# A graph network layer on one core: raw groups behind every second chunk of x, and SP fetching one tile of 48 by byte addresses

## The chip, the cores and the metric

The kernel runs on one core of a Trainium2 chip. The metric is device time in microseconds of one execution of the whole program on that core. Engines are PE (TensorE), DVE (VectorE), ACT (ScalarE), POOL (GpSimd) and SP (SyncE); in the profile a "q" behind an engine's name is its sequencer or queue (SPq: what SP issues).

## The reference

`x` has 12,500 rows of 256 features; there are 212,500 edges, sorted by `dst`, each with a source row `src` and 64 features of its own. All is float32.

```python
h = relu(layernorm(x))                                   # no scale or bias
messages = concat([h[src], edge_attr], axis=1) @ W_message   # 320 -> 256
agg = segment_sum(messages, dst)
n = layernorm(relu(agg) + h) * scale + bias
n = n + relu(n @ W0 + b0); n = n + relu(n @ W1 + b1); n = n + (n @ W2 + b2)
out = x + layernorm(h + n) * scale2 + bias2
```

## The kernel before, in words

**Tiles.** Nodes are 98 blocks of 128. Edges are 1,661 tiles of 128 edges, in 208 groups of 8 tiles (`G`). For a tile, 128 rows of `h` (1 KB each) are fetched by `src` into a slot of `ring` (64 slots, 8 groups, `RG`), with the 64 edge features beside them; PE multiplies the tile (128 x 320) by a one-hot matrix that DVE makes from `dst` and adds it to the block's sum in `acc_banks` (L628). When a block ends, about every 17 tiles, PE makes a visit (L519): the sums are multiplied by `W_message` and the block goes on through the layers, with DVE (L814) and ACT (L692).

**First stage.** x comes in 14 chunks of 896 KB (7 blocks each). DVE takes mean and variance (`x_moments`, L1030), ACT the root and then the normalised, rectified rows (`x_root`, `x_to_h`, L750 and L756), and SP stores the chunk to `h_table` in HBM (L370). The first four chunks are staged in the ring's upper half, the others in the five buffers of `xs`. Gathers from `h_table` can start only when all chunks are stored. Therefore the first 10 groups ("raw", `RAWS`) are gathered by POOL from x itself, 8 into the ring and 2 ("extra") into `xs` when its chunks are gone (L440), and are normalised in place, as units of the same pipeline. `UNITS` (L54) is the order: before, raw groups stand behind chunks 5 to 11 and 13, and two more at the end; 24 units. Beside the units DVE and ACT prepare the keys of the edges (`parts`, L1128; `keys`, L780). In its first stage SP asks for chunk n + 3 when chunk n is stored (L373).

**Main loop.** For the other groups each tile's rows come in one of two ways. POOL issues one indirect gather of 128 rows for a tile (`gather`, L433); its groups stand in the program one behind another. For the last tile of every eighth group, one tile of 64, SP fetches the rows: 128 single-row loads of 1 KB (L401), whose row numbers it loads into 32 registers four times (L398, L327). Those numbers are taken from `src` by 24 small loads before the loop (L391). SP also loads each group's edge features (`load_edges`, L340), which waits until PE has freed enough groups (`group_free`). A round of SP is eight edge loads and one tile of rows, 24 rounds (`MID`); then six groups ("tail") follow. POOL, too, waits for `group_free` before a group (L469). PE waits for each pair of tiles by `gathered`, for SP's tile by four semaphores `rows_in`, and for the edge features by `edges_in`. DVE waits for `group_free` before it makes the one-hots of a group two ahead.

**Order.** Each engine runs its own list in order; POOL's software queue q0, SP's queue q1 and ACT's q10 share 16 DMA engines. The end, for the last blocks, is written out (`pe_end`, L534; `act_end`; `dve_end`) and begins behind the last group.

Of the kernel before, what the change touches and what calls it, by code (L numbers as in the profile page):

```python
# [8 lines left out]
I32 = mybir.dt.int32  # L9
ALU = mybir.AluOpType  # L10
# [3 lines left out]
P = 128  # L14
D = 256
# [3 lines left out]
G = 8  # L19
# [3 lines left out]
BY_ROW = 32  # L23
XS = 5
# [15 lines left out]
def build(nc, x, src, dst, edges, w_message, w_mlp, feature_params, row_params, out, NB, XB, T):  # L40
# [44 lines left out]
    with ctx:  # L85
# [34 lines left out]
        xs = sb("xs", [P, XS, XB, D])  # L120
# [3 lines left out]
        xs_flat = xs[:, :, :, :].rearrange("p s b d -> p (s b d)")  # L124
        extra = xs_flat[:, 0:max(EG, 1) * G * F].rearrange("p (t f) -> p t f", f=F)
        rows_flat = xs_flat[0:1, 3 * XB * D:3 * XB * D + ROUNDS * P].bitcast(I32)
# [9 lines left out]
        row_src = rows_flat.rearrange("a (i p) -> a i p", p=P)  # L136
# [130 lines left out]
        rows_in = [sem(f"rows_in{c}") for c in range(P // BY_ROW)]  # L267
# [68 lines left out]
        def _(sp):  # L336
# [91 lines left out]
        def _(pool):  # L428
# [142 lines left out]
        def _(pe):  # L571
# [11 lines left out]
            def group(p, i, k, fetched, tiles=G):  # L583

                offset = {"raw": 0, "extra": RG, "SP": EG, "tail": EG, "later": 0}[fetched]
                g = i * RG + k + offset
# [3 lines left out]
                rhs = extra if fetched == "extra" else ring  # L590

                uses = i if fetched in ("SP", "tail") else (p - 1) * ROUNDS + i + 1 + MID + (1 if k < TAIL else 0)
                if fetched == "extra":
                    pe.wait_ge(extra_edges_in[k], 16)
                elif fetched == "raw":
                    pe.wait_ge(edges_in[k], 16)
                else:
                    pe.wait_ge(edges_in[k], (uses + 1) * 16)
# [4 lines left out]
                def rows_of(j):  # L603

                    slot = k * G + j
                    pair = slot // PT
# [6 lines left out]
                    if slot % PT:  # L613
                        return
                    if fetched == "SP" and pair == RG * PAIRS - 1:
                        pe.wait_ge(gathered[pair], uses * (16 * (PT - 1)))
                        return

                    short = 0
                    if k == TAIL - 1 and fetched != "SP":  # L620
                        short += PT - min(max(ENDS - j, 0), PT)
                    if pair == RG * PAIRS - 1:
                        short += MID
                    pe.wait_ge(gathered[pair], uses * (16 * PT) - short * 16)

                def tile(j):
                    at = steered[j]
                    return nc.tensor.matmul(acc_of(at), onehot[:, hot + j, :], rhs[:, k * G + j, :],  # L628
                                            start=False, stop=True, skip_group_check=True)

                def close():
                    pe.wait_ge(close_ready, visit + 1)
                    at = steered[AT]
                    sel = steered[VSEL]
                    closing = rhs[:, bass.ds(at + k * G, 1), :].rearrange("p a f -> p (a f)")
                    nc.tensor.matmul(acc_of(sel), close_hot[:, :], closing, start=False, stop=True,  # L636
                                     skip_group_check=True).then_inc(block_closed, 1)
# [23 lines left out]
            with nc.Fori(1, MID + 1, engines=[mybir.EngineType.PE], hint_back_edge=True) as i:  # L661
                for k in range(RG):
                    group(0, i, k, "SP")
            for k in range(TAIL):
                group(0, MID + 1, k, "tail", ENDS if k == TAIL - 1 else G)
# [82 lines left out]
        def _(act):  # L748
# [24 lines left out]
            def wrong_keys():  # L773
                act.wait_ge(rel_ready, 1)
                nc.scalar.activation(rel[:, :], rel[:, :], ACT.Relu, bias=highest[:, 0:1],
                                     accum_out=wrong[:, 0:1]).then_inc(wrong_ready, 1)
                nc.scalar.activation(below[:, :], below[:, :], ACT.Relu, scale=-1.0,
                                     accum_out=wrong[:, 1:2]).then_inc(wrong_ready, 1)
# [196 lines left out]
        def _(dve):  # L975
# [54 lines left out]
            def x_moments(u):  # L1030
# [8 lines left out]
                left = [] if u == 0 else list(range(5))  # L1039
                for k in range(count):  # L1040
                    rows_at = staged(n)[:, k, :] if kind == "chunk" else raw_tile(n, k)[:, 0:D]
                    op = nc.vector.bn_stats(x_stats[:, u % 2, k, :], rows_at)  # L1042
                    if k == count - 1:
                        op.then_inc(x_stats_ready, 1)
                    if u >= 1 and k == 0:
# [6 lines left out]
            def x_finish():  # L1052
                x_aggregate(len(UNITS) - 1)
                for k in range(5):
                    x_scale(len(UNITS) - 1, k)
# [15 lines left out]
            def check_keys():  # L1071
                dve.wait_ge(blocks_ready, 1)
                dve.wait_ge(dst_ready, 1)
                nc.vector.scalar_tensor_tensor(rel[:, :], blk[:, 1:T + 1], -float(P), dst_f[:, :], ALU.mult, ALU.add)
# [161 lines left out]
```

## Time and profile before

| | |
|---|---|
| median of 3 runs | 2134.97 us (2129.38 to 2136.38) |
| the profiled execution | 2135.35 us |
| its span, first to last instruction | 2133.5 us |
| mean granted TensorE clock | 0.905 |
| busy: PE, POOL, DVE, ACT | 1609.0, 1572.2, 967.5, 408.4 us |
| indirect gathers of POOL | 1,637 (80 from x, 1,557 from `h_table`) |
| single-row loads of SP | 3,072 (24 tiles) |

The span is followed from the first to the last instruction; the profiled time is 1.85 us longer. Times in the rows below are microseconds from the span's start, means and minima marked ns are nanoseconds. A busy share is an average over the stages; the first stage lasts to about 127 us, the main loop from there to about 2098, and the end to 2133.5.

### The profile page before, as it was taken

The page shows a single profiled execution, that of the slowest core. Times are in us where ns is not written, and L with a number is a line of the kernel's source. Part 1 is how long each engine was busy: PE and PEld are TensorE (multiplying, and loading weights), DVE is VectorE, ACT ScalarE, POOL GpSimd, SP SyncE. Part 2 cuts the span into 40 slices and gives each one's busy share as a digit, 9 for nine tenths or more (in the row PEclk, how much of TensorE's full clock was granted, in tenths as well). Part 3 has the DMA queues.
Part 4 walks back from the last instruction along what each step waited for, and adds up shares of the span by engine and source line. Part 5 has one row for each costly group of instructions (what it writes and reads, how often), then busy time and mean ns, then how long its engine had stood idle before and what let it go on. Part 6 is the DMA issues. An engine that isn't in the chain of part 4 may idle for free.

```text
span 2133.5 us, 41823 instructions
## 1 busy us (share of the span) xinstructions
PE 1609.0 (75%) x6722; PEld 1119.5 (52%) x6723; DVE 967.5 (45%) x4162; ACT 408.4 (19%) x1209; POOL 1572.2 (74%) x1645
## 2 busy tenths in 40 slices
PE   0059796697778769769769787878887887878886
PEld 0047574475456557547546555545555554545554
DVE  7866453353344344335335334434343434433445
ACT  5852111121111111111111111111111111111112
POOL 7657777777777777777777777777777777777772
PEclk9989997898888889879889889999999999999988
DMA  9796466556646646655664664665566466566461
GB/s 384 249 247 187 139 174 166 142 163 171 166 135 174 166 137 176 165 152 155 168 165 143 165 169 135 172 166 158 146 173 162 138 168 163 145 165 163 140 188 55
DMA packets 369326, 357.18 MB, mean 167 GB/s; under 512 B 256288, under 2 KB 312672, under 8 KB 369152
## 3 DMA queue, kind: packets, MB, share of 16 engines
q0 software_dynamic: 78576, 214.67, 35.3%
q1 hardware_dynamic: 233984, 89.44, 17.1%
q10 hardware_dynamic: 56592, 51.54, 7.7%
q14 instruction: 160, 1.31, 0.2%
q8 instruction: 14, 0.23, 0.0%
HBM read 329.01 MB, written 26.48 MB: 167 GB/s over the span
## 4 chain that ended last, share of the span: by engine, by line
POOL 42%; SPq 23%; issue 21%; PE 7%; DVE 2%; DMA 2%; ACT 2%; DVEq 0%; POOLq 0%; ACTq 0%
POOL ring L435 42%; SPq L401 16%; SPq L327 4%; PE acc_banks L628 3%; SPq L342 2%; ACT xs L761 1%; SPq L328 1%; PE agg_bank L504 1%; DMA xs<-x 1%; PE agg_bank L509 1%; PE y_bank L492 1%; DVE x_stats L1042 1%; ACT ring L761 1%; PE z_bank L492 1%; POOL xs L447 0%
## 5 line engine op out<-in xcount | busy, mean ns | idle before, releaser
L435 POOL DMA_INDIRECT ring<-h_table,src_all x1557 | 1491.7, 958 | 488.1 <-issue 471.8
L628 PE MATMUL acc_banks<-ring,onehot 128*128 128x320 f32 x3290 | 1027.4, 463 | 330.6 <-DMA ring<-h_table,src_all 161.2
L628 PEld LDWEIGHTS acc_banks<-ring,onehot 128*128 128x128 f32 x3290 | 634.2, 201 | 683.7 <-issue 487.7
L1159 DVE TENSOR_SCALAR onehot<-iota,dst_rel 128x128 f32<-128x128 f32 x1664 | 350.2, 296 | 353.0 <-PE acc_banks L628 325.4
L825 DVE TENSOR_TENSOR visit_rows<-agg_bank,visit_rows 128x256 f32<-128x256 f32 x98 | 41.6, 424 | 722.9 <-PE agg_bank L509 715.2
L678 ACT ACTIVATE uT<-z_bank,fp 128x128 f32<-128x128 f32 x196 | 78.9, 453 | 1266.4 <-PE z_bank L498 1261.5
L504 PE MATMUL agg_bank<-wm,ST 128*128 128x256 f32 (+1 forms) x582 | 172.0, 418 | 0.0
L504 PEld LDWEIGHTS agg_bank<-wm,ST 128*128 128x128 f32 (+1 forms) x582 | 110.7, 203 | 59.6 <-issue 40.0
L498 PE MATMUL z_bank<-ident,z 128*128 128x128 f32 x196 | 41.6, 297 | 104.5 <-DMA ring<-h_table 103.5
L684 ACT ACTIVATE r_bank<-y_bank,fp 128x128 f32<-128x128 f32 x196 | 58.6, 337 | 297.8 <-PE y_bank L492 297.8
L509 PE MATMUL agg_bank<-wl,u 128*128 128x256 f32 x392 | 114.5, 416 | 0.0
L492 PEld LDWEIGHTS y_bank<-u,wl 128*128 128x128 f32 x784 | 106.5, 198 | 5.8 <-issue 0.3
L492 PE MATMUL y_bank<-u,wl 128*128 128x128 f32 x784 | 106.9, 281 | 0.0
L492 PE MATMUL z_bank<-uT,wl 128*128 128x128 f32 x784 | 105.6, 279 | 0.0
L498 PEld LDWEIGHTS z_bank<-ident,z 128*128 128x128 f32 x196 | 29.3, 155 | 130.9 <-issue 114.0
L492 PEld LDWEIGHTS z_bank<-uT,wl 128*128 128x128 f32 x784 | 97.8, 196 | 0.0
L509 PEld LDWEIGHTS agg_bank<-wl,u 128*128 128x128 f32 x392 | 68.4, 195 | 39.1 <-issue 33.5
L435 POOL DMA_INDIRECT ring<-x,src_all x64 | 64.6, 1010 | 20.6 <-issue 19.2
L636 PE MATMUL acc_banks<-ring,close_hot 128*128 x192 | 75.6, 479 | 0.0
L684 ACT ACTIVATE r_bank<-z_bank,fp 128x128 f32<-128x128 f32 x196 | 58.6, 337 | 30.5 <-PE z_bank L492 27.8
L842 DVE TENSOR_TENSOR u<-u,r_bank 128x256 f32<-128x256 f32 x98 | 40.8, 416 | 17.9 <-ACT r_bank L684 17.1
L515 PE MATMUL st_bank<-ident,S_cur 128*128 128x128 f32 (+1 forms) x294 | 48.2, 273 | 0.0
(173 smaller groups left out, 1089.0 us busy)
## 6 DMA issues: line engine op xcount, KB each, us to landing
ring<-edges SPq DMA_DIRECT2D x206, 256.0 KB, 6.0
ring<-h_table SPq DMA_DIRECT2D x3072, 1.0 KB
ring<-h_table,src_all POOLq DMA_INDIRECT x1557
h_in<-h_table ACTq DMA_DIRECT2D x98, 128.0 KB
visit_rows<-h_table ACTq DMA_DIRECT2D x98, 128.0 KB
visit_rows<-x ACTq DMA_DIRECT2D x98, 128.0 KB
out<-o ACTq DMA_DIRECT2D x93, 128.0 KB
xs<-x SPq DMA_DIRECT2D x10, 896.0 KB, 10.8
```

The source lines that it names most:

```text
L327: eng.load(regs, table[0:1, bass.ds(start, len(regs))])
L401: sp.dma_start(ring[lane_at:lane_at + 1, RT - 1, 0:D], h_table[bass.ds(at[q], 1), :]).then_inc(rows_in[c], 16)
L435: nc.gpsimd.indirect_dma_start(out=ring[:, k * G + j, 0:D], out_offset=None, in_=rows, in_offset=bass.IndirectOffsetOnAxis(ap=src_all[:, g ...
L492: mm = nc.tensor.matmul(to[:, c * P:(c + 1) * P], wl[:, layer, k, c * P:(c + 1) * P], u[:, k * P:(k + 1) * P], start=(k == 0), stop=(k == 1))
L498: t = nc.tensor.transpose(to[:, c * P:(c + 1) * P], z[:, c * P:(c + 1) * P], ident[:, :])
L504: mm = nc.tensor.matmul(to, ST[0:m, c, :], wm[0:m, c, :], start=(c == 0), stop=(c == 2))
L509: mm = nc.tensor.matmul(to, u[:, k * P:(k + 1) * P], wl[:, 2, k, :], start=(k == 0), stop=(k == 1))
L628: return nc.tensor.matmul(acc_of(at), onehot[:, hot + j, :], rhs[:, k * G + j, :], start=False, stop=True, skip_group_check=True)
L636: nc.tensor.matmul(acc_of(sel), close_hot[:, :], closing, start=False, stop=True, skip_group_check=True).then_inc(block_closed, 1)
L678: op = nc.scalar.activation(uT[:, c * P:(c + 1) * P], zT[:, c * P:(c + 1) * P], ACT.Identity, scale=fp[:, 2, c:c + 1], bias=fp[:, 3, c:c + 1])
L684: op = nc.scalar.activation(r[:, c * P:(c + 1) * P], y[:, c * P:(c + 1) * P], ACT.Relu, bias=fp[:, layer, c:c + 1])
L1159: op = nc.vector.tensor_scalar(onehot[:, ((k + AHEAD) % OG) * G + j, :], iota[:, :], dst_rel[:, bass.ds((g + AHEAD) * G + j, 1)], None, AL ...
```

## The change

Two parts. **The first stage:** raw groups stand behind chunks 3, 5, 7, 9 and 11 (five), and the other five at the end; SP asks for chunk n + 4 when it has stored chunk n; unit 1 is finished at once (`EAGER`) instead of beside unit 2; the check of the keys is cut into an upper and a lower part, and the parts move to other units. **SP's tiles:** SP fetches the last tile of every sixth group, one of 48, so 32 tiles instead of 24, and POOL 1,549 instead of 1,557 from `h_table`. SP's and PE's loops run 8 times over three rounds (24 groups, four SP tiles) instead of 24 times over one. The row numbers of the 32 tiles are turned to byte offsets by one DVE shift, laid out by 32 small loads from SBUF, and a row load reads 1,024 bytes of `h_table` seen as bytes at an offset that is the register itself. Two semaphores in turn count a whole tile's rows.

```diff
+SP_EACH = 6
+ROW = 4 * D
...
-    MID = (NG - RAWS - 1) // RG
+    LOOP = 3 * RG
+    LOOPS = (NG - RAWS - 1) // LOOP
+    MID = LOOPS * 3
...
+    SP_TILES = MID * RG // SP_EACH
+    def by_sp(h):
+        return h % SP_EACH == SP_EACH - 1
+    SP_AT = {h % RG: h for h in range(LOOP) if by_sp(h)}
...
-        if n >= NX - 9 and n != NX - 2:
+        if n >= 3 and n % 2 == 1 and n < NX - 1:
             UNITS.append(("raw", sum(kind == "raw" for kind, _ in UNITS)))
     UNITS += [("raw", k) for k in range(sum(kind == "raw" for kind, _ in UNITS), RAWS)]
+    EAGER = (1,)
...
-                elif IN_RING + XS <= n + 3 < NX:
-                    sp.wait_ge(h_stored[buffer_of(n + 3)], 16 * (use_of(n + 3) - 1))
-                    load_x(n + 3)
+                elif IN_RING + XS <= n + 4 < NX:
+                    sp.wait_ge(h_stored[buffer_of(n + 4)], 16 * (use_of(n + 4) - 1))
+                    load_x(n + 4)
...
-            for i in range(1, MID + 1):
-                sp.dma_start(row_src[:, i, :], src[0:1, :, i * RT + RT - 1 + EG * G], allow_slow_non_contiguous=True).then_inc(row_src_in, 16)
-            sp.wait_ge(row_src_in, 16 * MID)
+            sp.wait_ge(src_bytes_ready, 1)
+            for n in range(SP_TILES):
+                sp.dma_start(rows_flat[:, n * P:(n + 1) * P], src_bytes[:, n:n + 1],
+                             allow_slow_non_contiguous=True).then_inc(row_src_in, 16)
+            sp.wait_ge(row_src_in, 16 * SP_TILES)
             row_regs = registers(nc.sync, BY_ROW)
-            def load_rows(i):
+            h_bytes = h_table.rearrange("r d -> (r d)").bitcast(U8)
+            def load_rows(n, slot, landed):
                 for c in range(P // BY_ROW):
-                    at = numbers(nc.sync, row_regs, rows_flat, i * P + c * BY_ROW, NB * P - 1)
+                    at = numbers(nc.sync, row_regs, rows_flat, n * P + c * BY_ROW, (NB * P - 1) * ROW)
                     for q in range(BY_ROW):
                         lane_at = c * BY_ROW + q
-                        sp.dma_start(ring[lane_at:lane_at + 1, RT - 1, 0:D], h_table[bass.ds(at[q], 1), :]
-                                     ).then_inc(rows_in[c], 16)
-            with nc.Fori(1, MID + 1, engines=[mybir.EngineType.SP], hint_back_edge=True) as i:
-                for k in range(RG):
-                    load_edges(k, i * RG + k + EG, i * RG + k + EG + 1)
-                load_rows(i)
+                        sp.dma_start(ring[lane_at:lane_at + 1, slot, 0:D].bitcast(U8),
+                                     h_bytes[bass.ds(at[q], ROW)].rearrange("(a n) -> a n", a=1)
+                                     ).then_inc(landed, 16)
+            with nc.Fori(0, LOOPS, engines=[mybir.EngineType.SP], hint_back_edge=True) as o:
+                for h in range(LOOP):
+                    k = h % RG
+                    load_edges(k, o * LOOP + RAWS + h, o * LOOP + RG + h + EG + 1)
+                    if by_sp(h):
+                        n = h // SP_EACH
+                        load_rows(o * len(SP_AT) + n, k * G + G - 1, rows_in[n % 2])
...
-                by_row = k == RG - 1 and g < NG - TAIL
+                by_row = by_sp(g - RAWS) and g < NG - TAIL
...
-                    if slot == RT - 1 and fetched == "SP":
-                        for c in range(P // BY_ROW):
-                            pe.wait_ge(rows_in[c], uses * (16 * BY_ROW))
-                        return
+                    if j == G - 1 and fetched == "middle" and by_sp(k):
+                        n = k // SP_EACH
+                        pe.wait_ge(rows_in[n % 2], (i * (len(SP_AT) // 2) + n // 2 + 1) * (16 * P))
...
-            with nc.Fori(1, MID + 1, engines=[mybir.EngineType.PE], hint_back_edge=True) as i:
-                for k in range(RG):
-                    group(0, i, k, "SP")
+            with nc.Fori(0, LOOPS, engines=[mybir.EngineType.PE], hint_back_edge=True) as o:
+                for h in range(LOOP):
+                    group(0, o, h, "middle")
...
-            keys = {5: blocks_of_tiles, 6: destinations, 8: wrong_keys}
+            keys = {6: blocks_of_tiles, 7: destinations, 10: upper_keys, 12: lower_keys}
             x_root(0)
             x_to_h(0)
-            x_root(1)
-            for u in range(2, len(UNITS)):
+            for u in range(1, len(UNITS)):
                 x_root(u)
-                x_to_h(u - 1)
+                if u - 1 not in (0,) + EAGER:
+                    x_to_h(u - 1)
+                if u in EAGER:
+                    x_to_h(u)
...
+            def byte_addresses():
+                dve.wait_ge(src_in, 16)
+                nc.vector.tensor_scalar(src_bytes[:, :], src_all[:, RAWS + SP_EACH - 1:RAWS + MID * RG:SP_EACH, G - 1],
+                                        (ROW - 1).bit_length(), None, ALU.logical_shift_left).then_inc(src_bytes_ready, 1)
...
-            parts = {2: cast_iotas, 4: shift_lasts, 7: check_keys, 10: relative_keys, 11: closing_places, 12: steering,
-                     14: lambda: first_onehots(0), 16: lambda: first_onehots(1)}
+            parts = {2: cast_iotas, 4: shift_lasts, 9: check_upper, 11: check_lower, 14: relative_keys, 15: closing_places,
+                     16: steering, 17: lambda: first_onehots(0), 18: lambda: first_onehots(1)}
             for u in range(len(UNITS)):
                 x_moments(u)
+                if u in EAGER:
+                    x_finish(u)
                 if u in parts:
                     parts[u]()
-            x_finish()
+            x_finish(len(UNITS) - 1)
+            byte_addresses()
             second_layer()
```

## Rows read from the trace of the kernel before

**Rows 1.** The page: packets of SP's queue q1; the chain, by line.

```profile
q1 hardware_dynamic: 233984, 89.44, 17.1%
...
POOL ring L435 42%; SPq L401 16%; SPq L327 4%; PE acc_banks L628 3%; SPq L342 2%; ACT xs L761 1%; SPq L328 1%; PE agg_bank L504 1%; DMA xs<-x 1%; PE agg_bank L509 1%; PE y_bank L492 1%; DVE x_stats L1042 1%; ACT ring L761 1%; PE z_bank L492 1%; POOL xs L447 0%
```

**Rows 2.** The costliest groups (line, engine, operation | busy, mean ns | idle, releasers); POOL in one window.

```profile
L435 POOL DMA_INDIRECT ring<-h_table,src_all x1557 | 1491.7, 958 | 488.1 <-issue 471.8 <-PE acc_banks L628 8.4 <-DMA h_table<-xs 7.8
...
160.00:2080.00 1920.00, 1456.07 (x1523) 0.90 0.59 160
```

**Rows 3.** Timeline of POOL: start us, us, engine line op [idle before <-releaser].

```profile
153.24 0.94 POOL L435 DMA_INDIRECT ring<-h_table,src_all  x1 [6.27 <-PE acc_banks L628]
...
2098.21 0.95 POOL L435 DMA_INDIRECT ring<-h_table,src_all  x1 [0.30 <-issue]
```

**Rows 4.** Timeline of SP's queue: start us, us, line, tile, count (432.51 cut at 460).

```profile
140.05 17.66 SPq L391 DMA_DIRECT2D xs<-src  x24
161.72 38.61 SPq L342 DMA_DIRECT2D ring<-edges  x8
203.45 61.93 SPq L401 DMA_DIRECT2D ring<-h_table  x128
...
357.43 61.52 SPq L401 DMA_DIRECT2D ring<-h_table  x128
...
432.51 27.59 SPq L401 DMA_DIRECT2D ring<-h_table  x60
...
1975.85 61.73 SPq L401 DMA_DIRECT2D ring<-h_table  x128
```

**Rows 5.** Waits of POOL: us in total, times, longest us.

```profile
POOL xs L447 <- DMA h_table<-xs: 13.7, 3, 9.4
```

**Rows 6.** Chain of waits, 0 to 130 us: start us, us, what.

```profile
118.47 5.73 DMA xs<-x,src_all
```

**Rows 7.** Timeline of ACT in the first stage: one raw unit.

```profile
49.37 4.02 ACT L761 ACTIVATE ring<-ring,x_shift,x_rstd 128x256 f32<-128x256 f32 x8
```

**Rows 8.** Lines L401 and L342 of SP: op, count, ns min/median/max.

```profile
L401 SPq MOVE ring<-h_table x3072: 29/29/38, 203.4 to 2037.3; - x192
L401 SPq DMA_DIRECT2D ring<-h_table x3072: 224/228/312, 203.4 to 2037.4; - x192
L401 SPq FUSED_REGOPS  x2976: 37/37/53, 203.8 to 2037.2; - x199
...
L342 SPq MOVE ring<-edges x192: 29/29/36, 161.6 to 1972.4; - x192
```

**Rows 9.** Chain of waits, 203 to 206 and 262 to 281 us.

```profile
203.96 0.23 SPq L401
...
204.38 0.23 SPq L401
...
266.17 0.42 SPq L342
...
271.44 1.41 SPq L342
...
274.79 1.70 SPq L342
...
279.56 0.31 SPq L401
```

**Rows 10.** Timeline of PE: the start of one visit and of the next.

```profile
146.62 0.44 PE L498 MATMUL z_bank<-ident,z 128*128 128x128 f32 x2 [1.08 <-DVE z L859]
...
160.87 0.38 PE L498 MATMUL z_bank<-ident,z 128*128 128x128 f32 x2
```

**Rows 11.** Windows: us, PE, PEld, DVE, ACT, POOL busy (x), PE clock, DMA share, GB/s.

```profile
1015.00:1031.00 16.00, 2.52 (x7) 1.96 (x8) 0.00 (x0) 1.24 (x3) 12.04 (x14) 0.50 0.49 126
```

**Rows 12.** Timeline of PE at the end.

```profile
2103.49 3.39 PE L628 MATMUL acc_banks<-ring,onehot 128*128 128x320 f32 x12
```

More of the change, by code:

```diff
@@ L9 @@
 I32 = mybir.dt.int32
+U8 = mybir.dt.uint8
 ALU = mybir.AluOpType
@@ L119, in build @@
         blk = sb("blk", [P, T + 1])
-        xs = sb("xs", [P, XS, XB, D])
+        xs_flat = sb("xs", [P, XS * XB * D + D])
+        xs = xs_flat[:, 0:XS * XB * D].rearrange("p (s b d) -> p s b d", b=XB, d=D)
         h_end, x_end, hb_end = xs[:, 2, 0:LAG, :], xs[:, 3, 0:LAG, :], xs[:, 4, 0:LAG, :]
-        xs_flat = xs[:, :, :, :].rearrange("p s b d -> p (s b d)")
         extra = xs_flat[:, 0:max(EG, 1) * G * F].rearrange("p (t f) -> p t f", f=F)
-        rows_flat = xs_flat[0:1, 3 * XB * D:3 * XB * D + ROUNDS * P].bitcast(I32)
+        rows_flat = xs_flat[0:1, EG * G * F:EG * G * F + SP_TILES * P].bitcast(I32)
+        src_bytes = sb("src_bytes", [P, SP_TILES], I32)
         def staged(n):
@@ L135, in raw_tile @@
             return ring[:, n * G + j, :] if n < RG else extra[:, (n - RG) * G + j, :]
-        row_src = rows_flat.rearrange("a (i p) -> a i p", p=P)
         flat = onehot[:, :, :].rearrange("p j f -> p (j f)")
@@ L266, in build @@
         row_src_in = sem("row_src_in")
-        rows_in = [sem(f"rows_in{c}") for c in range(P // BY_ROW)]
+        src_bytes_ready = sem("src_bytes_ready")
+        rows_in = [sem(f"rows_in{c}") for c in range(2)]
         gathered = [sem(f"gathered{q}") for q in range(RG * PAIRS)]
@@ L583, in group @@
             def group(p, i, k, fetched, tiles=G):
-                offset = {"raw": 0, "extra": RG, "SP": EG, "tail": EG, "later": 0}[fetched]
-                g = i * RG + k + offset
+                offset = {"raw": 0, "extra": RG, "middle": RAWS, "tail": RAWS + MID * RG, "later": 0}[fetched]
+                g = i * (LOOP if fetched == "middle" else RG) + k + offset
                 steered = numbers(nc.tensor, regs, steer_flat, g * W, *[1] * G, G - 1, 1, T)
@@ L590, in group @@
                 rhs = extra if fetched == "extra" else ring
-                uses = i if fetched in ("SP", "tail") else (p - 1) * ROUNDS + i + 1 + MID + (1 if k < TAIL else 0)
+                slot = k % RG
+                if fetched == "middle":
+                    uses = i * 3 + k // RG + 1
+                elif fetched == "tail":
+                    uses = MID + 1
+                else:
+                    uses = (p - 1) * ROUNDS + i + 1 + MID + (1 if k < TAIL else 0)
                 if fetched == "extra":
@@ L597, in group @@
                 else:
-                    pe.wait_ge(edges_in[k], (uses + 1) * 16)
+                    pe.wait_ge(edges_in[slot], (uses + 1) * 16)
                 pe.wait_ge(onehots, p * NG + g + 1)
@@ L603, in rows_of @@
                 def rows_of(j):
-                    slot = k * G + j
-                    pair = slot // PT
                     if fetched in ("raw", "extra"):
                         return
-                    if slot == RT - 1 and fetched == "SP":
-                        for c in range(P // BY_ROW):
-                            pe.wait_ge(rows_in[c], uses * (16 * BY_ROW))
-                        return
[L613 to L616, printed above, removed]
+                    pair = slot * PAIRS + j // PT
+                    last = j // PT == PAIRS - 1
+                    if j == G - 1 and fetched == "middle" and by_sp(k):
+                        n = k // SP_EACH
+                        pe.wait_ge(rows_in[n % 2], (i * (len(SP_AT) // 2) + n // 2 + 1) * (16 * P))
+                    if j % PT:
                         return
                     short = 0
-                    if k == TAIL - 1 and fetched != "SP":
+                    if slot == TAIL - 1 and fetched != "middle":
                         short += PT - min(max(ENDS - j, 0), PT)
-                    if pair == RG * PAIRS - 1:
-                        short += MID
-                    pe.wait_ge(gathered[pair], uses * (16 * PT) - short * 16)
+                    if last and slot in SP_AT and fetched == "middle":
+                        first = (k // RG + 1) * PT - (1 if k >= SP_AT[slot] else 0)
+                        pe.wait_ge(gathered[pair], i * (16 * (3 * PT - 1)) + first * 16)
+                    else:
+                        if last and slot in SP_AT:
+                            short += LOOPS
+                        pe.wait_ge(gathered[pair], uses * (16 * PT) - short * 16)
                 def tile(j):
                     at = steered[j]
-                    return nc.tensor.matmul(acc_of(at), onehot[:, hot + j, :], rhs[:, k * G + j, :],
+                    return nc.tensor.matmul(acc_of(at), onehot[:, hot + j, :], rhs[:, slot * G + j, :],
                                             start=False, stop=True, skip_group_check=True)
@@ L634, in close @@
                     sel = steered[VSEL]
-                    closing = rhs[:, bass.ds(at + k * G, 1), :].rearrange("p a f -> p (a f)")
+                    closing = rhs[:, bass.ds(at + slot * G, 1), :].rearrange("p a f -> p (a f)")
                     nc.tensor.matmul(acc_of(sel), close_hot[:, :], closing, start=False, stop=True,
@@ L660, in _ @@
                 group(0, 0, e, "extra")
-            with nc.Fori(1, MID + 1, engines=[mybir.EngineType.PE], hint_back_edge=True) as i:
-                for k in range(RG):
-                    group(0, i, k, "SP")
+            with nc.Fori(0, LOOPS, engines=[mybir.EngineType.PE], hint_back_edge=True) as o:
+                for h in range(LOOP):
+                    group(0, o, h, "middle")
             for k in range(TAIL):
-                group(0, MID + 1, k, "tail", ENDS if k == TAIL - 1 else G)
+                group(0, 0, k, "tail", ENDS if k == TAIL - 1 else G)
             with nc.tensor.If(passes < 2):
@@ L771, in destinations, with upper_keys @@
                 nc.scalar.activation(dst_f[:, :], dst_i[:, :], ACT.Copy).then_inc(dst_ready, 1)
-            def wrong_keys():
+            def upper_keys():
                 act.wait_ge(rel_ready, 1)
@@ L1038, in x_moments @@
                     dve.wait_ge(x_moments_ready, u - 1)
-                left = [] if u == 0 else list(range(5))
+                done = u == 0 or u - 1 in EAGER
+                left = [] if done else list(range(5))
                 for k in range(count):
@@ L1044, in x_moments @@
                         op.then_inc(x_stats_ready, 1)
-                    if u >= 1 and k == 0:
+                    if not done and k == 0:
                         x_aggregate(u - 1)
@@ L1050, in x_moments, with x_finish @@
                     x_scale(u - 1, k)
-            def x_finish():
-                x_aggregate(len(UNITS) - 1)
+            def x_finish(u):
+                x_aggregate(u)
                 for k in range(5):
-                    x_scale(len(UNITS) - 1, k)
+                    x_scale(u, k)
             def cast_iotas():
@@ L1068, in shift_lasts, with check_upper, check_lower @@
                 nc.vector.tensor_scalar(last_i[:, :], last_i[:, :], P.bit_length() - 1, None, ALU.arith_shift_right).then_inc(lasts_ready, 1)
-            def check_keys():
+            def check_upper():
                 dve.wait_ge(blocks_ready, 1)
                 dve.wait_ge(dst_ready, 1)
-                nc.vector.scalar_tensor_tensor(rel[:, :], blk[:, 1:T + 1], -float(P), dst_f[:, :], ALU.mult, ALU.add)
+                nc.vector.scalar_tensor_tensor(rel[:, :], blk[:, 1:T + 1], -float(P), dst_f[:, :], ALU.mult, ALU.add).then_inc(rel_ready, 1)
+            def check_lower():
                 nc.vector.scalar_tensor_tensor(below[:, :], blk[:, 0:T], -float(P), dst_f[:, :], ALU.mult, ALU.add).then_inc(rel_ready, 1)
```

2 lines of the change are left out of this document (added).

## The prediction

> **What bounds the kernel now.** I read the page's chain first, then the costliest groups, then the timelines of POOL and SP. The chain goes through POOL's gathers for 42% and through SP's row loads at L401 for 16%, and through PE's matmuls for 3% [rows 1], so two feeders are close to each other. The reader is to see which one sets the pace. POOL issues 1,557 gathers from `h_table`, back to back, with no wait but 0.30 us of issue between two [rows 2, 3]. From 160 to 2080 us it issues 1,523 in 1,920 us, **1.261 us each** [rows 2]. It waits for PE only 8.4 us in all, 6.27 of them once, at 153.24 [rows 2, 3]. From there (1,557 - 16) x 1.261 gives 2096.5; the last gather starts at 2098.21 [rows 3]. So POOL sets the end: the sum closes without PE.
>
> SP is close behind. Its 64-tile round is 61.9 us for the 128 single rows of one tile, 10.3 for eight edge loads (266.17 to 276.49), and 4 for the loop branch and the first load of row numbers: 76.1 from 203.45 to 279.56, 75.1 from 357.43 to 432.51 [rows 4, 9]. POOL's 63 gathers take 79.4. SP starts late and catches up: its last tile starts 23 rounds after 203.45, at 1975.85, 77.1 each [rows 4], which is over its 75.1 by waits for PE. Slack: 4 us in 79, so 5%.
>
> **Part 1: the start.** Among its 16 extra raw gathers POOL waits 13.7 us for stores of `xs` chunks, three times [rows 5]. The last extra gather lands 5.73 after 118.47 [rows 6], and from there the chain runs over ACT and DVE to PE's third group, for which POOL waits until 153.24: 29 us that the change leaves alone. With raw groups behind chunks 3, 5, 7, 9 and 11 only, chunk 9 is unit 12 instead of 13, chunk 10 is 14 instead of 15, chunk 11 is 15 instead of 17, and chunk 13 is 18 instead of 20. Two raw units (4.02 us of ACT each, beside its root [rows 7]) go behind the last chunk; x is asked for one chunk sooner; and the key checks are split, so that DVE and ACT wait less for each other. Bounds: the whole 13.7 and one more raw unit at most, 18; 5 if ACT and DVE, which still have the same 24 units, become the limit. I take **12 us**: the waits nearly gone, the same units behind them. PE's first groups, SP's loads and POOL's restart all move by it.
>
> **Part 2: fewer gathers on POOL.** SP takes 32 tiles instead of 24, so POOL issues 8 fewer: 8 x 1.261 = 10.1 us. For 48 tiles POOL needs 47 x 1.261 = **59.3 us**.
>
> **Part 3: SP.** A row before is a FUSED_REGOPS of 37 ns (row number to byte offset), a MOVE of 29 and a DMA issue of 228 [rows 8]; the chain shows a start every 0.41 us (203.96, 204.38 [rows 9]), which leaves 0.116 for three gaps, some 0.04 each. With byte addresses nothing is to be multiplied, so I take the FUSED_REGOPS away with its 0.04. The MOVE stays: it stands before every load with a register in its address, the edge loads' too [rows 8]. A row is then 0.41 - 0.078 = 0.332. Per tile 31 x 4 = 124 such instructions go (the first of each 32 shares one with the number handling): 61.6 (the later tiles: 61.73 at 1975.85 [rows 4]) - 9.7 = 51.9. The other terms for 48 tiles: six edge loads, 266.17 to 272.85 in the chain, 6.7 [rows 9] (they cost more from the third on, so six cost less than six eighths of a burst, but not 0.4 each); the first load of 32 numbers with its handling, 276.49 to 279.56, 3.1 [rows 9]; 0.3 of gaps and a third of a loop branch less often. Sum 51.9 + 6.7 + 3.1 + 0.3 = 62.0 from a round of 76.1; typical rounds are 0.5 to 1 shorter, so **61.5 us, 2.2 more than POOL's 59.3**. Bounds for the row: 0.26, if the MOVE (29 + 41 ns) goes as well, to 0.41, if nothing does.
>
> Where the removed instruction's 41 ns gap is counted, the page "Perfetto Trace Analysis" of the Trainium skill (Sequencer-only Instruction) bears: the profiler's span of a sequencer instruction leaves out fetch and push, a hidden tail. By that the tail goes with the instruction, as I count; with the reported 37 ns alone the period would be 66.6 and the end some 158 us later.
>
> **Small edits.** SP loads 32 columns of addresses instead of 24 (17.66 us for 24 [rows 4], so 5.9 more), before its first loop. Cover: its next eight edge loads are stretched to 38.61 us by PE's pace, against 10.3 [rows 4, 9]; its first tile now sits at group 15, two groups or 14.2 us of PE sooner (visits start at 146.62 and 160.87 [rows 10]), so 28.3 - 14.2 - 5.9 = 8 us are left. If that cover went, the whole loop would start later by what is missing. DVE's one shift to bytes is behind the last raw unit, as `second_layer` is: 0.2 us. PE's waits change only their counts.
>
> **The sum.** PE lets SP begin its first tile at 203.45 - 14.2 - 12 = 177.3; it is issued at 229. With 2.2 us lost in each of 31 periods, POOL is ahead by one ring at first and absorbs it, then it waits for groups that wait for SP's rows. SP's last tile ends at 229 + 31 x 61.5 = 2135.7, against 2037.6 before [rows 4]. Behind it PE has 45 tiles at 14.2 per 17 [rows 10], 37.6; a colder clock after its wait and the landing, 6 (PE's granted clock is 0.50, its lower level of 1.2 GHz, from 1015 to 1031, where it mostly waits, with 2.5 us busy [rows 11]); and from the last matmul of L628, 2106.9, to the end, 26.6 [rows 12]. Span 2135.7 + 70.2 = 2205.9. The profiled execution took 2135.35 for a span of 2133.5, so 2207.7, and it stands 0.4 above the median of the runs: **2208 us**, 3.4% slower. POOL's 22 us are not seen. The case's own range: 62 or 61 for the period is 31 x 0.5 = 16 either way, the start 6 either way: 2185 to 2230.
>
> **Rivals.**
> *POOL stays the bound; faster.* SP's period needs only to be under 59.3: a row of 0.315 or less. With the MOVE gone too it is 0.26, the period about 53, and SP has 6 us of slack. For it: the issue alone is 0.228 [rows 8], the cost of edge loads spaced out is not shown, and 2.2 us is 4% of my sum of terms. Against: every register address in the trace has its MOVE, and edge loads in a burst cost 1.4 us by the sixth and 1.7 by the eighth [rows 9]. Then both parts count in full: 2135.35 - 12 - 10.1 = 2113; with the start's bounds 2105 to 2122. Chance 0.38.
> *SP bound, as forecast:* 0.52.
> *Nearly level.* A period of 59.5 to 60: the gain is given back late in the run, 2125 to 2145. Chance 0.05.
> *The bytes save nothing.* The offset still passes through an instruction, a row stays at 0.41 and the period is 71.2: 9.7 x 31 = 301 more than forecast, about 2509. For it: the trace has no byte-wide address. Chance 0.05. No row here shows it: the q1 packets, 233,984, leave under 21,000 beside the 208 x 1,024 of the edges [rows 1], so the rows of 256 elements are not split now, and a sixteenfold split of 3,072 would be 49,152. An issue as dear as the first edge load of a burst, 0.42 us [rows 9], would make a row over 0.5, later still.
>
> **How the numbers follow.** The time is that of the likeliest case. The range starts at the bottom of the POOL case and ends at the top of the SP case, 2105 to 2228, which leaves out some 0.15 (the byte case and the edges of the others). A measurement here can tell 0.3%, 6.4 us, from no change. Faster: 0.38 of the POOL case and a little of the level one, 0.39. Same 0.04. Slower 0.57.
>
> **What would show it.** FUSED_REGOPS at the line of the row loads: about none, MOVE still there; a row every 0.33 us; a tile's 128 rows in 52; SP tiles 61 to 62 apart with no wait of SP for PE. POOL waits for PE: from 8.4 us to some 90. POOL's first `h_table` gather about 112 to 117 and its 17th about 141. PE's longest waits at the SP tiles. If POOL is still back to back to the end, with its last gather near 2076, the forecast is wrong and the row was cheaper than 0.315; if the tiles are 71 apart, the byte form saved nothing.

## The result, and the profile after

The kernel after takes **2212.10 us** (median of 4 runs, 2210.47 to 2214.05), beside 2133.77 for the kernel before in the same runs: a ratio of **1.0372**, 95% interval 1.0356 to 1.0388. The forecast was 2208, slower; it was right in sign and within 4.1 us. The profiled execution took 2210.47 us for a span of 2209.0.

The page of the kernel after: busy engines, SP's queue, the chain by engine and line, and the costliest groups.

```profile
PE 1555.4 (70%) x6722; PEld 1132.7 (51%) x6723; DVE 967.8 (44%) x4163; ACT 408.9 (19%) x1209; POOL 1564.2 (71%) x1637
...
q1 hardware_dynamic: 237184, 90.49, 16.6%
...
SPq 73%; issue 17%; PE 4%; DVE 3%; ACT 2%; DMA 1%; DVEq 0%; ACTq 0%; POOLq 0%
...
L455 POOL DMA_INDIRECT ring<-h_table,src_all x1549 | 1481.7, 957 | 543.0 <-issue 471.7
L653 PE MATMUL acc_banks<-ring,onehot 128*128 128x320 f32 x3290 | 958.8, 450 | 280.3 <-DMA ring<-h_table 219.4
...
L518 PE MATMUL z_bank<-ident,z 128*128 128x128 f32 x196 | 42.3, 301 | 272.9 <-DMA ring<-h_table 271.1
```

The chain went through POOL for 42% and the row loads for 16% [rows 1]; now SP's queue has 73% of it. q1 has 3,200 packets more than before [rows 1], 1,024 of them the rows of eight more tiles. A row in byte form is still one packet: with two, the 4,096 rows alone would have added over 4,096, and `no_bytes` below, which loads the same rows by their numbers, has the same 237,184. PE waits 490.5 us for SP's rows (219.4 + 271.1), at its 32 tiles, 15.3 each: it is done with everything else and stands before that one tile.

SP's timeline (start us, us, line, tile, count): the start, two periods, and the last tile.

```profile
129.46 23.50 SPq L405 DMA_DIRECT2D xs<-src_bytes  x32
157.17 19.99 SPq L355 DMA_DIRECT2D ring<-edges  x6
180.28 50.87 SPq L417 DMA_DIRECT2D ring<-h_table  x128
231.41 7.47 SPq L355 DMA_DIRECT2D ring<-edges  x6
241.93 50.87 SPq L417 DMA_DIRECT2D ring<-h_table  x128
293.07 6.42 SPq L355 DMA_DIRECT2D ring<-edges  x6
...
2088.01 50.81 SPq L417 DMA_DIRECT2D ring<-h_table  x128
```

From 180.28 to 2088.01 are 31 periods, **61.54 us** each. SP waits for no engine in them; it issues. POOL's timeline (the first, the 17th and the last gather from `h_table`) says the same from the other side.

```profile
113.66 0.95 POOL L455 DMA_INDIRECT ring<-h_table,src_all  x1 [5.01 <-DMA h_table<-xs]
...
144.24 0.94 POOL L455 DMA_INDIRECT ring<-h_table,src_all  x1 [10.89 <-PE acc_banks L653]
...
2132.40 0.95 POOL L455 DMA_INDIRECT ring<-h_table,src_all  x1 [0.30 <-issue]
```

The 17th gather from `h_table` (144.24) starts 9.0 us sooner than before and the last one 34.2 later [rows 3], with 8 fewer between them. The waits of SP, POOL and PE (us in total, times, longest):

```profile
SPq L355 <- PE acc_banks L653: 19.6, 5, 9.2
```

```profile
POOL ring L455 <- PE acc_banks L653: 66.3, 21, 10.9
```

SP waits for PE five times, all in all 19.6 us, and never between the first row of its first tile and its last tile. POOL waits for PE 66.3 us, where it had 8.4 [rows 2]. The instructions of the row loads (ns min/median/max):

```profile
L417 SPq MOVE ring<-h_table x4096: 29/29/37, 180.2 to 2138.5; - x196
L417 SPq DMA_DIRECT2D ring<-h_table x4096: 224/225/387, 180.3 to 2138.6; - x196
```

No FUSED_REGOPS is left at the row loads; MOVE and issue are as in [rows 8].

### The profile page after: what moved, and what is told of

It reads as the page before. It is cut to its first block, busy times and chain, and to the rows that moved or that the text cites. A ratio compares the mean times of both kernels' runs of the same rounds, so it can differ in the third digit from the quotient of the medians.

```text
span 2209.0 us, 40952 instructions
## 1 busy us (share of the span) xinstructions
PE 1555.4 (70%) x6722; PEld 1132.7 (51%) x6723; DVE 967.8 (44%) x4163; ACT 408.9 (19%) x1209; POOL 1564.2 (71%) x1637
## 4 chain that ended last, share of the span: by engine, by line
SPq 73%; issue 17%; PE 4%; DVE 3%; ACT 2%; DMA 1%; DVEq 0%; ACTq 0%; POOLq 0%
SPq L417 48%; SPq L340 12%; SPq L355 9%; SPq L341 3%; PE acc_banks L653 2%; DVE x_stats L1073 1%; DMA ring<-x 1%; ACT xs L786 1%; ACT ring L786 1%; PE agg_bank L524 0%; PE agg_bank L529 0%; DMA xs<-x,src_all 0%; DVE x_mv L1056 0%; PE y_bank L512 0%; SPq L354 0%
## 5 line engine op out<-in xcount | busy, mean ns | idle before, releaser
L653 PE MATMUL acc_banks<-ring,onehot 128*128 128x320 f32 x3290 | 958.8, 450 | 280.3 <-DMA ring<-h_table 219.4
L653 PEld LDWEIGHTS acc_banks<-ring,onehot 128*128 128x128 f32 x3290 | 641.6, 198 | 562.5 <-issue 332.5
L518 PE MATMUL z_bank<-ident,z 128*128 128x128 f32 x196 | 42.3, 301 | 272.9 <-DMA ring<-h_table 271.1
L524 PE MATMUL agg_bank<-wm,ST 128*128 128x256 f32 (+1 forms) x582 | 179.1, 432 | 0.0
L529 PEld LDWEIGHTS agg_bank<-wl,u 128*128 128x128 f32 x392 | 69.4, 197 | 40.4 <-issue 34.5
```

Of the source, the lines that this page charges most:

```text
L524: mm = nc.tensor.matmul(to, ST[0:m, c, :], wm[0:m, c, :], start=(c == 0), stop=(c == 2))
L529: mm = nc.tensor.matmul(to, u[:, k * P:(k + 1) * P], wl[:, 2, k, :], start=(k == 0), stop=(k == 1))
```

## The experiments

Five questions, ten kernels, two of them run twice. "Before" is the kernel before in the same job.

**1. The two parts apart.** `a_only` is the kernel before with the diff of the first stage alone (the new `UNITS`, `EAGER`, the cut key parts, x asked for at n + 4); `b_only` is the kernel before with SP's part alone (its x loads and units as before).

> The kernel before with the change of the first stage alone (order of the raw groups, x asked for sooner, the split key checks). Theory 1: POOL stays the bound and everything moves by the 9.0 us by which its 17th gather came sooner: 2133.8 - 9.0 = 2125. Rival: SP's first tile or PE's order takes it back in the loop, 2134.

Measured: 2126.74 us (2124.96 to 2128.49), before 2136.99, ratio 0.9957, interval 0.9943 to 0.9971.

> The kernel before with SP's part alone (one tile of 48, byte addresses, loops of three rounds), the first stage as before. Theory 1: SP's tiles 61.5 apart, all of it shifted late by the 9 us of the start: 2212 + 9 = 2221. Rival: part of the loss comes from the new first stage, then nearer 2200.

Measured: 2220.66 us (2218.17 to 2222.28), before 2138.12, ratio 1.0386, interval 1.0370 to 1.0402. SP's first tile starts at 190.13 here and at 180.28 with both parts, 9.9 us sooner, and the times differ by 8.6. So the first stage gives 8.6 to 10.2 us whichever feeder sets the pace, and the whole loss lies in SP's part. Both runs came out as expected under theory 1.

**2. Is it the number of rows that SP issues?** `rows124` and `rows116` leave rows out of every SP tile.

```diff
-                    for q in range(BY_ROW):
+                    for q in range(BY_ROW if c < 3 else 28):       # rows124; rows116 has 20
```

> The changed kernel with 124 of the 128 single-row loads per SP tile; the rows of four lanes of each SP tile are left out (stale values are multiplied in their place). Theory 1 (SP sets the pace: its tiles are 61.5 us apart where POOL needs 59.3): four rows of 0.32 us go from each of 31 periods, 1.3 x 31 = 40, so 2172 us, SP tiles 60.3 apart. Theory 2 (something else that came with the three-round loop sets it: PE's visits behind its waits, a colder clock, or the DMA engines): within 0.3% of 2212.

Measured: 2171.38 us (2169.40 to 2171.46), before 2136.99, ratio 1.0164 (1.0147 to 1.0181). 128 rows fewer took 40.7 us off, **0.318 us a row**; the two medians are from different jobs, whose kernels before differ by 3 us, so this is good to 0.03 or so. The trace says it without that: the first and the last tile start at

```profile
179.51 49.43 SPq L417 DMA_DIRECT2D ring<-h_table  x124
...
2047.63 49.48 SPq L417 DMA_DIRECT2D ring<-h_table  x124
```

which is a period of 60.26 instead of 61.54, and four rows are 4 x 0.319 = 1.28. Every row of SP is on the path.

> The same with 116 of 128 rows; the rows of twelve lanes of each SP tile are left out. Theory 1: 3.9 us go from a period, 57.7 would be under POOL's 59.3, so POOL becomes the bound: before's 2133.8 less 9 (start) less 10.1 (8 gathers) = 2115 us, not 2212 - 120 = 2092; SP tiles 59.3 apart, with waits of SP for PE, and POOL's waits for PE back to about 12 us. Theory 2: about 2212.

Measured: 2115.82 us (2113.08 to 2120.19), ratio 0.9903 (0.9886 to 0.9919). 384 rows at 0.319 would be 122 us; it took only 96, because POOL takes over: its waits for PE (us, times, longest) are nearly gone. SP's tiles are not 59.3 apart, as was expected, but 57.60, with no wait of SP among them: SP begins behind POOL and is still catching up, and its last tile is issued by 2011.43.

```profile
POOL ring L455 <- PE acc_banks L653: 12.9, 9, 10.4
```

```profile
179.24 46.72 SPq L417 DMA_DIRECT2D ring<-h_table  x116
...
1964.72 46.71 SPq L417 DMA_DIRECT2D ring<-h_table  x116
```

This is the forecast's rival "POOL stays the bound", 2113 us, made real by taking 3.9 us from SP's period.

The two runs also show where the bound changes. The kernel after is 96.3 us above `rows116`, 3.11 for each of 31 periods, so SP would have to be at 61.54 - 3.11 = 58.4 us to be level with POOL; `rows124` gives 60.26 - 55.6 / 31 = 58.5. That is 0.8 to 0.9 below POOL's 59.3 (an estimate from these two distances).

**3. What the byte addresses do.** `no_bytes` loads row numbers and lets the address be worked out at the row load, as before (the shift is by 0 there; the row load is shown).

```diff
-  sp.dma_start(ring[lane_at:lane_at + 1, slot, 0:D].bitcast(U8),
-               h_bytes[bass.ds(at[q], ROW)].rearrange("(a n) -> a n", a=1)
+  sp.dma_start(ring[lane_at:lane_at + 1, slot, 0:D], h_table[bass.ds(at[q], 1), :]
```

> The changed kernel with row numbers in place of byte addresses in SP's row loads. Theory 1: a FUSED_REGOPS of 37 ns returns before each row, rows 0.41 us apart, 124 x 0.088 = 10.9 us per tile, tiles 72.4 apart, 31 x 10.9 = 338 us more: 2550. Theory 2, if SP were not the pace: about 2212.

Measured: 2529.98 us (two runs, 2529.52 and 2530.44), ratio 1.1846 (1.1822 to 1.1870). The instruction is back, the other two are unchanged:

```profile
L416 SPq MOVE ring<-h_table x4096: 29/29/38, 180.4 to 2456.1; - x196
L416 SPq DMA_DIRECT2D ring<-h_table x4096: 224/225/312, 180.4 to 2456.2; - x196
L416 SPq FUSED_REGOPS  x3968: 37/37/53, 180.8 to 2456.0; - x199
```

A row is 0.406 us against 0.319: the instruction of 37 ns costs 0.087. The period is 71.42, 9.9 more, which over 31 periods, with the last tile's 11.0, is the difference of 317.9 us. The expectation, 2550, had 10.9 us a period: the rows cost that, but the burst of edge loads got 1.2 cheaper (last section). The byte form does what it was made for; the kernel still loses because of what it was given in return.

**4. How many tiles SP can carry.** `three24` gives SP 3 tiles in 24 groups (24 in all, as before), `seven48` 7 in 48 groups (28 in all).

```diff
-        return h % SP_EACH == SP_EACH - 1
+        return h % LOOP in SP_HS      # three24: [5, 14, 23]; seven48: [5, 12, 18, 25, 32, 39, 46], LOOP = 6 * RG
```

> The changed kernel with three SP tiles per 24 groups instead of four (groups 5, 14, 23 of a loop, bytes and loops of three rounds kept). Theory 1: SP has over 15 us of slack per round, POOL is the bound with its 1,557 gathers: 2125, as the first stage's change alone. Rival (the loop of three rounds or byte loads cost by themselves): slower than that by more than 6.

Measured: 2127.11 us (2124.95 to 2128.79), before 2138.12, ratio 0.9955 (0.9940 to 0.9970). That is `a_only` (0.9957) again: with 24 tiles the cheaper row buys nothing, because POOL sets the pace.

> The changed kernel with seven SP tiles per 48 groups (28 tiles, 1,553 gathers; spacings of 56 tiles and once of 48). Theory 1: SP needs 50.6 + 3.3 + about 9.5 = 63.4 per 56 tiles, POOL 55 x 1.261 = 69.4: POOL is the bound, four gathers fewer than three of 24: 2125 - 5 = 2120. Rival: irregular places stall POOL, 2130 or more.

Measured: **2119.35 us** (2115.86 to 2120.50), ratio **0.9912** (0.9897 to 0.9927). It beats both kernels. The ratio is 0.9955 with 24 tiles already; four gathers fewer account for 5.0 of the other 7.8 us. The chain has gone back to POOL:

```profile
POOL 51%; issue 20%; SPq 14%; PE 6%; DVE 3%; DMA 3%; ACT 2%; POOLq 0%; DVEq 0%; ACTq 0%
```

```profile
POOL ring L456 <- PE acc_banks L654: 13.1, 9, 10.6
```

This share without byte addresses was not run. By an estimate it would not do: `no_bytes` takes 71.42 us for one tile and six edge loads, and POOL needs 55 x 1.261 = 69.4 for 56 tiles. So the cheaper row is what makes room for the 28 tiles, though not for 32.

**5. Can SP's period be cut with all 32 tiles?** The edge loads of a burst get dearer towards its end: by place in it they are issued in 0.41, 0.40, 0.81, 1.19, 1.59 and 1.46 us (means of the 31 bursts between SP's tiles), 5.85 in sum. (The 5.97 of the expectations below counts the six loads behind the last tile as a 32nd burst.) `spread` issues them two by two before the first three runs of 32 rows, each load a whole period ahead; the first six stand before the loop.

```diff
+                    def ahead(c):
+                        for e in ((1, 2), (3, 4), (5, 6), ())[c]:
+                            load_edges((h + e) % RG, o * LOOP + RAWS + h + e, o * LOOP + RG + h + e + EG + 1)
+                    load_rows(o * len(SP_AT) + n, h % RG * G + G - 1, rows_in[n % 2], ahead)
```

> The changed kernel with the six edge loads of a period issued two by two between the four runs of 32 rows, one tile ahead, instead of in one burst. Theory 1a (an edge load is dear only behind others in the queue: 0.40 us for the first two, 0.81 to 1.59 from the third): six cost 6 x 0.65 = 3.9 us instead of 7.6, the period is 58, under POOL's 59.3, and the end is POOL's: 2115. Theory 1b (descriptor making costs the same wherever it stands, the next rows pay): period 61.5, 2212.

Measured: **2370.11 us** (2363.35 to 2371.49), ratio 1.1074 (1.1058 to 1.1090). Both expectations are wrong. The issues did get cheap: here one line of the edge loads (ns min/median/max) of the kernel after and the same of `spread`:

```profile
L355 SPq DMA_DIRECT2D ring<-edges x206: 372/816/3212, 93.9 to 2149.0; - x103
```

```profile
L355 SPq DMA_DIRECT2D ring<-edges x206: 367/399/2934, 93.4 to 2270.2; - x103
```

But SP's timeline of `spread` shows a pair that takes 12 us, and its waits say why:

```profile
1014.64 23.85 SPq L418 DMA_DIRECT2D ring<-h_table  x64
1038.75 12.07 SPq L355 DMA_DIRECT2D ring<-edges  x2
1053.86 10.73 SPq L418 DMA_DIRECT2D ring<-h_table  x32
...
SPq L355 <- PE acc_banks L653: 270.7, 58, 11.6
```

An edge load waits for PE to free its slot in a ring of eight groups. A load six groups ahead of the tile needs PE to have passed the second group before that tile; PE has just stood still for SP's last tile, so SP now waits for what PE does behind that wait. Two engines that had overlapped wait for each other in turn. The sum closes: issues 5.85 - 6 x 0.438 = 3.22 us less in a period; of the 270.7 us of waits 237.7 fall between the first and the last tile, where the kernel after has none, 7.67 a period; 61.54 - 3.22 + 7.67 = 66.0, measured 66.12. The first tile starts at 194.12, 13.8 later, after 33.0 us of such waits instead of 18.6. And 31 x 4.58 + 13.8 = 156 of the 158 us lost.

Two more kernels take this apart: `ahead_burst` has all six edge loads of the next tile ahead, in one burst; `spread_late` has them between the rows and none ahead, nor any before the loop.

```diff
-                        for e in ((1, 2), (3, 4), (5, 6), ())[c]:
+                        for e in ((1, 2, 3, 4, 5, 6), (), (), ())[c]:      # ahead_burst
+                        for e in ((0, -5, -4), (-3, -2), (-1,), ())[c]:    # spread_late
```

> The change with the six edge loads of a stretch taken apart but none of them ahead of the row tile that they belong to: three (the sixth, the first, the second) before the first 32 rows, two (the third, the fourth) before the second 32, one (the fifth) before the third 32, none before the last. Both theories of why the variant with edge loads a tile ahead was slow are put to it. (1) Being ahead was the harm: each edge load waits until PE has freed its slot of a ring of eight groups, so a load six groups ahead of the rows makes SP wait for PE, which has just waited for SP's rows. Here no load is ahead, so the wait does not come, and the dearer issues of a burst go: by place in the burst they took 410, 436, 872, 1232, 1582, 1437 ns in the change, sum 5.97 us; here 410 + 436 + 872 + 410 + 470 + 410 = 3.0 us, so SP's period falls from 61.5 to some 58.5 us, under the 59.3 of POOL (47 gathers at 1.261), which then sets the pace: 2120 us, between 2112 and 2145, with SP waiting for slots some 1 us a period. (2) Standing between the runs of rows is the harm (rows slowed behind an edge load, or edges landing too late for PE): then the period rises over 61.5 here too: 2230 us or more.

> The change with the six edge loads of a stretch in one burst as before, but one row tile ahead: those of the next stretch stand before this tile's rows. (1) Being ahead is the harm: the last of the six waits until PE has freed the second group before this tile's own, five groups after the last row tile. In the variant with the pairs one tile ahead the first load of a freed slot went out 7.1 us after the last row, and two groups more took some 14.5 us, so the last one goes out at 7 + 4 x 7.4 = 36.7 us; then 0.5 us, 3.05 to the first row and 50.6 of rows: period 90.8 us in place of 61.5, and 205 + 31 x 90.8 + 50.8 + 75 = 3145 us, between 2950 and 3250. (2) If being ahead costs nothing and the standing between the rows was the harm: 2212 us as the change, or less.

Both fell on a chip on which the kernel before itself took 3557.25 us instead of 2135: 3427.85 us for `spread_late` and 4267.33 for `ahead_burst`. They were run once more, and fell on the same chip (before 3617.26).

> The same kernel as spread_late, whose runs fell on a chip on which the kernel before took 3557 us in place of 2135, so that its 0.9643 says nothing in figures. (1) Being a tile ahead was the harm of the variant with spread edge loads: here none is ahead, six issues cost some 3.0 us a tile in place of 5.97, SP's period falls from 61.5 to some 58.5 us, under POOL's 59.3, and the time is 2120 us, between 2112 and 2145. One thing may keep it above that: the fourth and fifth edge loads now go out 15 and 29 us into the stretch, and if PE is there before them it waits for edges (on the slow chip it did, 45 times); SP does not wait for PE, so this costs only what exceeds PE's slack of some 15 us a stretch. (2) Standing between the runs of rows was the harm: 2230 us or more.

> The same kernel as ahead_burst, whose runs fell on the chip on which the kernel before took 3557 us; there it took 840 us more than the spread variant with none ahead. (1) Being ahead is the harm: as worked out for ahead_burst, the last of six edge loads goes out 36.7 us after the last row, the period is 90.8 us, the time 3145 us, between 2950 and 3250. (2) If being ahead costs nothing: 2212 us or less.

Measured: 3506.41 us (3491.67 to 3512.76) and 4331.27 us (4322.79 to 4332.85); ratios to before 0.9689 (0.9627 to 0.9751) and 1.1965 (1.1896 to 1.2035), and in the first job 0.9643 and 1.1997. None of the expected times can be held against these. What can be read is the wait: in `ahead_burst2` SP waits for PE

```profile
SPq L355 <- PE acc_banks L653: 1407.6, 105, 23.6
```

with a whole burst of six taking 48.76 us in its timeline,

```profile
1022.81 48.76 SPq L355 DMA_DIRECT2D ring<-edges  x6
```

and `spread_late2` has no wait of L355 for PE at all; on one chip they differ by 825 us (4331.27 - 3506.41). That a load ahead brings the wait is shown by that, and by `spread` on an ordinary chip, where the sum above closes without any price for the place between the rows. Whether `spread_late` would bring the period from 61.54 to 58.4, where POOL takes over, stays **open**; its 0.9643 and 0.9689 were measured where the bound was another: rows in the first job's profile were issued 0.585 us apart in the mean (0.322 in the median), PE waited for late edges too, and the kernel after was not run there.

## Why the prediction was right, point by point

**The bound before: POOL, with SP 5% behind.** Right: `three24` makes SP's rows cheaper at the same number of tiles and gains nothing over `a_only`.

**The start, 12 us.** Right in kind, oversized. POOL's wait for stores among its extra gathers went from 13.7 [rows 5] to 0.3 us, and its first gather from `h_table` came at 113.66. But the 17th, which waits for PE's third group, came only 9.0 us sooner, and stood 10.89 us for it. Where the rest went stands in the chain of the kernel after (start us, us, what):

```profile
99.59 3.45 ACT xs L786 x7
...
103.05 4.60 DMA h_table<-xs
...
107.71 7.55 DMA xs<-x,src_all
```

The last extra gather goes out as soon as the store of a chunk has landed, and it is waited for from 107.71 for 7.55 us, where it was 5.73 from 118.47 [rows 6]. It was issued 10.8 us sooner, landed 1.8 slower, and so was there 8.9 us sooner; PE's first visit comes 9.0 sooner, at 137.62 instead of 146.62 [rows 10]. The units behind it took what they took before. `a_only` measured 10.2 us in all.

**The row, 0.332 us.** Measured 0.319 in the median. The FUSED_REGOPS took not 37 + 41 but 87 ns with it, so the rows of a tile take 50.87 us in the timeline, not 51.9: 1.0 less. That a hidden part goes with the instruction was counted rightly, and it is the larger part. Here the Trainium skill's page "Perfetto Trace Analysis" (Sequencer-only Instruction) agreed: beside the reported 37 ns, 50 more that no row shows go with the instruction.

**The rest of the period, 10.1 us, less the 0.5 that typical rounds are shorter: 9.6.** Measured 61.54 - 50.87 = 10.67, so 1.1 more. The burst of six edge loads was put at 6.7 from the first six of a burst of eight [rows 9]; it takes 7.22 in the mean (7.47 and 6.42 in the timeline above). The other half is the 0.5 allowed for typical rounds, which did not show. The two errors cancelled, 51.9 + 9.6 = 61.5 against 50.87 + 10.67 = 61.54. That the period fits to 0.04 us is luck; its parts were each off by 1.

**The end.** First tile foreseen at 177.3, measured 180.28. Of these 3.0 us, 2.1 are the start (12 foreseen, 9.9 by `b_only`'s 190.13). The other 0.9 is a misreading: 14.2 us is PE's time for a visit and 17 tiles, and the first SP tile moved by two groups, 16 tiles; `b_only` shows 203.45 - 190.13 = 13.3. Last tile's end foreseen at 2135.7, measured 2138.8. From there to the span's end 70.2 foreseen, 70.2 measured, again by two parts that cancel: the matmuls of L653 end with

```profile
2180.41 3.39 PE L653 MATMUL acc_banks<-ring,onehot 128*128 128x320 f32 x12
```

45.0 us behind SP's last row (43.6 foreseen), and 25.2 are left behind them (26.6). The step that carried the risk was the cover of the 32 small loads: they took 23.50 us, as foreseen (17.66 + 5.9), and SP's first edge loads behind them still stretch to 19.99 us by PE's pace, so the cover held.

**The rival that POOL stays the bound** had 0.38, and its condition was wrong: a period under POOL's 59.3, a row of 0.315 or less. The forecast's own sum, with 59.3 in it, gives 229 + 31 x 59.3 + 70.2 = 2137.5 for the span, not 2111: SP starts its first tile late, and behind its last one PE still has 45 tiles to do, so SP has to be faster than POOL to make that good. The runs put the change at 58.4, and with the burst as dear as it is the row would have had to be 0.295 (3.11 us over 128 rows is 0.024). The measured 0.319 is thus further from that rival than 4 ns. `rows116` shows the case: 2115.8 us. The same slip is in the level rival: periods of 59.5 to 60 give 2146 to 2161 by the forecast's sum, not 2125 to 2145; `rows124`, with 60.26, took 2171.4. **The rival that the bytes save nothing** was put at 2509; `no_bytes` is 2530. Of the 21 us, 9.9 are the rows of one tile more, which 31 x 9.7 leaves out (there are 32 tiles), 6.8 the period (71.42 for 71.2) and 3.1 the later first tile. The rule on a copy split by its outermost dimension, which stood beside it in the Trainium skill ("DMA: Bandwidth & Descriptors", Why a DMA increments its semaphore by 16 and not by 1), did not make itself felt: q1 has 3,200 packets more in all, where 4,096 rows split in sixteen would be 65,536.

**The signs named ahead** were seen: no FUSED_REGOPS, MOVE still there, tiles 61 to 62 apart, POOL waiting for PE (66 us instead of "some 90"), the 17th gather at 144 instead of 141.

## What to carry to other kernels

Where two engines feed a third in fixed shares, work out each one's period for its share from per-item rows, to the half per cent; moving one more item from the fuller to the slacker engine can turn a slack of 5% into a deficit of 4%, and the whole deficit is paid in every period. Equal periods are not enough for the engine that starts later or has more work behind its last item: compare start + periods + what follows the last item for both. Here the kernel after lost 31 x 2.24 = 69.4 us to POOL's pace and 26.9 more by this, 96.3 in all. Choose the share by those sums (here 7 tiles in 48 groups instead of 8), not by how much cheaper one item became. A load that is issued ahead of its turn behind a wait on the consumer can close a loop between producer and consumer: before moving it, count the slots of the ring and ask which group the consumer must have passed.

## What had not been expected of the hardware

- FUSED_REGOPS, an instruction of SP's sequencer reported at 37 ns, takes 87 ns of its time (0.406 - 0.319 us a row, medians over 4,096 rows in `no_bytes` and the kernel after).
- Edge loads (256 KB, 128 x 8 pieces of 256 bytes) issued behind one another are not evenly dear. One burst of the kernel after, in its chain of waits (start us, us):

```profile
231.41 0.41 SPq L355
...
232.08 0.39 SPq L355
...
232.73 1.66 SPq L355
...
234.64 0.69 SPq L355
...
235.57 2.23 SPq L355
...
238.06 0.82 SPq L355
```

  Two go at 0.4 us and the later ones take up to 2.23; in `spread`, with 32 rows between pairs, the mean is 0.44, and the rows behind them are not slowed (0.321 us apart in the median). With the slower rows of `no_bytes` before it, the burst of six takes 5.98 us in place of 7.22.
- On one chip the kernel before took 1.67 and 1.69 times its time elsewhere. In `spread_late` there SP's MOVE at the row loads took up to 1,407 ns, against at most 37 in the kernel after:

```profile
L418 SPq MOVE ring<-h_table x4096: 1/29/1407, 273.2 to 3351.5; - x196
```

  Neither row says why, and the cause is left open.
